# Flamingo cross-attention with a routed feed-forward: the fold's u in 48 jobs over the batches' borders, and m stored in longer and loaded in shorter packets

## The reference, cut to what matters

```python
# x (4, 2048, 512), ctx (4, 77, 512); 16 heads of 64
xn = layernorm(layernorm(x), gamma, beta)
q = (xn @ w_q) per head;  k, v = split(ctx @ w_kv) per head
attn = softmax(q * 64**-0.5 @ k.T)                    # 77 keys per head
x = x + tanh(g_xattn) * tanh(gate) * (attn @ v @ w_out + b_out)
y = layernorm(x)
probs = softmax(y @ gate_w.T + gate_b); top 2 of 10 (8 experts, 2 null), weights of true ones normalised
x = x + tanh(g_ffn) * sum over chosen e of weight * (y @ expert_w[e] + expert_b[e])
```

## Time and profile before

| what | value |
|---|---|
| median of 3 runs | 1552.9 us |
| the profiled execution's own time | 1539.97 us |
| its span in the trace | 1538.2 us |
| TensorE busy | 1336.4 us (87%) |
| VectorE busy | 1204.0 us (78%) |
| ScalarE busy | 785.8 us (51%) |
| GpSimd busy | 921.5 us (60%) |

### The profile page before, as it was taken

How to read it: one execution, slowest core, us unless ns; L and a number is a source line. 1 busy time by engine, 2 the same in 40 slices (tenths; PEclk the granted TensorE clock), 3 DMA queues, 4 the chain that set the end, 5 groups by cost and what they waited for, 6 DMA issues and landing times. The chain is left out here.

```text
span 1538.2 us, 31337 instructions
## 1 busy us (share of the span) xinstructions
PE 1336.4 (87%) x7241; PEld 685.0 (45%) x7242; DVE 1204.0 (78%) x2764; ACT 785.8 (51%) x2777; POOL 921.5 (60%) x781
## 2 busy tenths in 40 slices
PE   5676199999999999999999999998039998899997
PEld 4332054444444444444444444544015554455553
DVE  5766478899999999999999999996356775666765
ACT  5766266655555555565555555554024443344442
POOL 0450255557666766766776776674537775666664
PEclk9787699999999999999999999999569999999999
DMA  5795468889887788887788987777135442677773
GB/s 199 195 241 166 136 128 179 179 189 217 180 238 163 179 191 215 213 195 171 172 206 198 235 182 167 172 155 174 63 131 169 161 155 101 212 239 238 238 235 116
DMA packets 419892, 280.37 MB, mean 182 GB/s; under 512 B 325009, under 2 KB 352785, under 8 KB 419448
## 3 DMA queue, kind: packets, MB, share of 16 engines
q1 hardware_dynamic: 391992, 205.52, 55.1%
q0 software_dynamic: 27840, 74.18, 15.3%
HBM read 123.38 MB, written 83.07 MB: 134 GB/s over the span
## 5 line engine op out<-in xcount | busy, mean ns | idle before, releaser
L752 PE MATMUL scores<-m_sb,zT 128*128 (+2 forms) x2304 | 416.4, 339 | 43.3 <-DMA zT<-z_parts 31.2
L768 PE MATMUL mix<-u_sb,pT 128*128 128x512 f16 (+1 forms) x1920 | 425.0, 379 | 0.6 <-DVE x_out L947 0.6
L841 ACT ACTIVATE expd<-scores,less 128x77 f32<-128x77 f32 x1024 | 317.4, 329 | 203.4 <-DVE less L923 202.5
L1582 PE MATMUL out_bank<-w_parts,y_columns 128*128 x1440 | 335.7, 384 | 2.3 <-issue 2.2
L752 PEld LDWEIGHTS scores<-m_sb,zT 128*128 128x128 f16 x2304 | 223.6, 98 | 212.1 <-DMA zT<-z_parts 31.6
L768 PEld LDWEIGHTS mix<-u_sb,pT 128*128 128x128 f16 (+1 forms) x1920 | 187.8, 98 | 220.5 <-DVE x_out L947 0.8
L841 ACT ACTIVATION_READ_ACCUMULATOR expd<-scores,less 128x1 f32 x1024 | 213.9, 209 | 0.0
L1582 PEld LDWEIGHTS out_bank<-w_parts,y_columns 128*128 128x128 f16 x1440 | 142.2, 99 | 152.2 <-issue 13.6
L1247 POOL DMA_INDIRECT table<-payload,row_i x128 | 158.6, 1239 | 59.2 <-issue 34.7
L1605 ACT CAST y_columns<-yT_bank 128x512 f16<-128x512 f32 x120 | 70.2, 585 | 183.9 <-PE yT_bank L1569 183.9
L1224 POOL TENSOR_TENSOR z<-z,beta 128x512 f32<-128x512 f32 x64 | 152.0, 2376 | 5.0
(11 more groups left out here) (158 smaller groups left out, 1880.1 us busy)
## 6 DMA issues: line engine op xcount, KB each, us to landing
comb<-x_out SPq DMA_DIRECT2D x64, 512.0 KB, 3.2
x_ln<-in_x_dram SPq DMA_DIRECT2D x64, 256.0 KB, 2.7
x_res<-in_x_dram SPq DMA_DIRECT2D x64, 256.0 KB, 2.8
w_raw<-in_L_ffn_expert_w_dram SPq DMA_DIRECT2D x64, 128.0 KB, 2.3
m_dram<-m_stage SPq DMA_DIRECT2D x32, 231.0 KB, 5.7
u_dram<-m_sb SPq DMA_DIRECT2D x48, 154.0 KB
m_sb<-m_dram SPq DMA_DIRECT2D x12, 616.0 KB
u_sb<-u_dram SPq DMA_DIRECT2D x6, 1024.0 KB, 6.8
```

What stands on the lines that cost most here:

```text
L752: last = pe.matmul(scores[s][k][:, 0:n], zT[:, s, zp, t, :], m, start=(t == 0 and (zp, mp) == PRODUCTS[0]), stop=(t == DT - 1 and (zp, mp) ...
L768: last = pe.matmul(mix[:], pT[0:n, s, pp, k, :], u_sb[0:n, k, up, :], start=(k == 0 and (pp, up) == PRODUCTS[0]), stop=(k == KT - 1 and (p ...
L841: last = act.activation(expd[:, s, h * KEYS:(h + 1) * KEYS], scores[s][k][:, at:at + KEYS], ACT.Exp, bias=less[:, s, h:h + 1], scale=1.0 / ...
L1582: last = pe.matmul(c.out_bank[s][:], yT[:, s, yp, t, :], w_parts[:, bass.ds(e, 1), t, wp, :].rearrange("p a n -> p (a n)"), start=(t == 0 ...
```

## The change

It changes how u is cut into jobs and how m lies in DRAM.

- The four batches' 308 rows of one head lie side by side in `v_stack`. They are now cut at 128, so a head has three jobs, of 128, 128 and 52 rows, and the 16 heads have 48 jobs, ordered by head. A job's rows belong to up to three batches, and `u_pieces` cuts the store where a batch ends: job 0 holds the 77 rows of batch 0 (into `u_sb`, cut as before) and 51 of batch 1; job 1 holds 26 of batch 1, 77 of batch 2 and 25 of batch 3; job 2 holds 52 of batch 3. The slots get 128 rows.
- `m_dram` is laid out by row block, part, quad, row, batch, so that one store of a quad's part is 128 rows of 3·308·2 = 1848 contiguous bytes in place of 384 of 616 B. `m_stage` has the part ahead of the batch. The load of one batch's m takes two DMAs a row block, one for each part, of 512 pieces of 616 B each, in place of one DMA with 128 pieces of 4928 B. PE's count of landed loads is doubled.

```diff
 def load_m(engine, m_sb, m_dram, b, t):
-    return engine.dma_start(m_sb[:, :, t].rearrange("p a l c -> p (a l) c"),
-                            m_dram[bass.ds(b, 1), :, t].rearrange("a p l c -> (a p) l c"))
+    for part in range(2):
+        yield engine.dma_start(m_sb[:, :, t, part].rearrange("p a (q c) -> p (a q) c", q=QUADS),
+                               m_dram[t, part, :, :, bass.ds(b - 1, 1)].rearrange("q p a c -> p (q a) c"))
...
-    NU = BATCH * HEADS
+    CHUNKS = -(-CK // P)
+    NU = HEADS * CHUNKS
...
-        m_stage = sb("m_stage", [P, MS, BATCH, 2, 4 * KEYS], F16)
+        m_stage = sb("m_stage", [P, MS, 2, BATCH, 4 * KEYS], F16)
...
+        def chunk_rows(n):
+            return min(P, CK - n % CHUNKS * P)
...
         def u_pieces(n):
-            b, h = divmod(n, HEADS)
-            if b > 0:
-                return [(slice(0, KEYS), u_dram[b, h * KEYS:(h + 1) * KEYS])]
...
+            h, c = divmod(n, CHUNKS)
+            pieces = []
+            for b in range(BATCH):
+                first, end = max(b * KEYS, c * P), min((b + 1) * KEYS, c * P + chunk_rows(n))
+                if first >= end:
+                    continue
+                s0, s1 = first - c * P, end - c * P
+                row0, row1 = h * KEYS + first - b * KEYS, h * KEYS + end - b * KEYS
+                if b > 0:
+                    pieces.append((slice(s0, s1), u_dram[b, row0:row1]))
+                    continue
+                for k in range(row0 // P, (row1 - 1) // P + 1):
+                    p0, p1 = max(row0 - k * P, 0), min(row1 - k * P, P)
+                    j0, j1 = k * P + p0 - row0 + s0, k * P + p1 - row0 + s0
+                    pieces.append((slice(j0, j1), u_sb[p0:p1, k]))
             return pieces
...
-                sp.dma_start(m_sb[:, 0, dt, :, cols], m_stage[:, g % MS, 0]).then_inc(m_stored[g % MS], 16)
+                sp.dma_start(m_sb[:, 0, dt, :, cols], m_stage[:, g % MS, :, 0]).then_inc(m_stored[g % MS], 16)
                 for part in range(2):
-                    sp.dma_start(m_dram[1:, :, dt, part, cols].rearrange("b p c -> p b c"),
-                                 m_stage[:, g % MS, 1:, part]).then_inc(m_stored[g % MS], 16)
+                    sp.dma_start(m_dram[dt, part, quad], m_stage[:, g % MS, part, 1:]).then_inc(m_stored[g % MS], 16)
...
                 for part in range(2):
-                    last = pe.matmul(out[0:KEYS, :], v_stack[:, h, b * KEYS:(b + 1) * KEYS],
+                    last = pe.matmul(out[0:m, :], v_stack[:, h, c * P:c * P + m],
                                      kvw_parts[:, h // 4, part, h % 4, :], start=(h > 0 and part == 0), stop=(part == 1))
...
-    m_dram = nc.dram_tensor("m_dram", [BATCH, P, DT, 2, COLS], F16, kind="Internal").ap()
+    m_dram = nc.dram_tensor("m_dram", [DT, 2, QUADS, P, BATCH - 1, 4 * KEYS], F16, kind="Internal").ap()
```

More of the change, by code:

```diff
@@ L27 @@
 COLS = HEADS * KEYS
+QUADS = HEADS // 4
 KT = -(-COLS // P)
@@ L122, in fold_context @@
         v_stack = sb("v_stack", [P, HEADS, CK], F16)
-        m_stage = sb("m_stage", [P, MS, BATCH, 2, 4 * KEYS], F16)
-        u_stage = m_sb[0:KEYS, 1].rearrange("p t l c -> p (t l c)")[:, 0:US * 2 * D].rearrange(
+        m_stage = sb("m_stage", [P, MS, 2, BATCH, 4 * KEYS], F16)
+        u_stage = m_sb[:, 1].rearrange("p t l c -> p (t l c)")[:, 0:US * 2 * D].rearrange(
             "p (u l n) -> p u l n", u=US, l=2)
@@ L129, in fold_context @@
         bias_parts = sb("bias_parts", [1, 2, D], F16)
-        ones_row = sb("ones_row", [1, KEYS], F16)
+        ones_row = sb("ones_row", [1, P], F16)
         gates = sb("gates", [P, 2])
@@ L184, in job @@
                 cols = slice(hh * KEYS, (hh + 1) * KEYS)
-                hi = m_stage[:, g % MS, :, 0, cols]
-                return [(hi, m_stage[:, g % MS, :, 1, cols], hi,
+                hi = m_stage[:, g % MS, 0, :, cols]
+                return [(hi, m_stage[:, g % MS, 1, :, cols], hi,
                          bank[:, 0:CK].rearrange("p (b j) -> p b j", b=BATCH),
                          M_SCALE * DH ** -0.5 / (K_SCALE * W16))]
-            u = (n - U0) % US
-            return [(u_stage[:, u, 0], u_stage[:, u, 1], u_stage[:, u, 0], bank[0:KEYS, :], u_gain[0:KEYS, :])]
+            u, m = (n - U0) % US, chunk_rows(n - U0)
+            return [(u_stage[0:m, u, 0], u_stage[0:m, u, 1], u_stage[0:m, u, 0], bank[0:m, :], u_gain[0:m, :])]
+        def chunk_rows(n):
+            return min(P, CK - n % CHUNKS * P)
         def u_pieces(n):
-            b, h = divmod(n, HEADS)
-            if b > 0:
-                return [(slice(0, KEYS), u_dram[b, h * KEYS:(h + 1) * KEYS])]
[L198 to L202, removed]
+            h, c = divmod(n, CHUNKS)
[13 more added lines that the diff above has]
+                    pieces.append((slice(j0, j1), u_sb[p0:p1, k]))
             return pieces
@@ L321, in _ @@
             for n in range(NU):
[L322 to L326, removed]
+                h, c = divmod(n, CHUNKS)
+                if c == 0 and h % 4 == 0:
+                    pe.wait_ge(chunk_hi_ready, 4 + h // 4 + 1)
+                    pe.wait_ge(wout_lo_ready, h // 4 + 1)
+                out, m = bank(U0 + n), chunk_rows(n)
                 if h == 0:
                     for part in range(2):
-                        pe.matmul(out[0:KEYS, :], ones_row[:], bias_parts[:, part], start=(part == 0), stop=False)
+                        pe.matmul(out[0:m, :], ones_row[:, 0:m], bias_parts[:, part], start=(part == 0), stop=False)
                 for part in range(2):
-                    last = pe.matmul(out[0:KEYS, :], v_stack[:, h, b * KEYS:(b + 1) * KEYS],
+                    last = pe.matmul(out[0:m, :], v_stack[:, h, c * P:c * P + m],
                                      kvw_parts[:, h // 4, part, h % 4, :], start=(h > 0 and part == 0), stop=(part == 1))
@@ L718, in batch @@
                     if not last:
-                        load_m(sp, m_sb[:, bass.ds((b + 1) % 2, 1)], m_dram, b + 1, k).then_inc(m_in, 16)
+                        for load in load_m(sp, m_sb[:, bass.ds((b + 1) % 2, 1)], m_dram, b + 1, k):
+                            load.then_inc(m_in, 16)
                     step(i0 + TPB - 4 + k, k % 2)
@@ L742, in score @@
                     if later(i, TPB):
-                        pe.wait_ge(m_in, 16 * DT * (i // TPB))
+                        pe.wait_ge(m_in, 32 * DT * (i // TPB))
                 for k in banks:
```

## The result

The changed kernel takes 1560.6 us, the median of 20 runs (1553.1 to 1568.2), against 1553.65 of the kernel before in 20 runs beside it (1549.9 to 1562.2). The ratio is 1.0046, 95% interval 1.0031 to 1.0061: slower by 7 us, within the 1% that I called no change. In a later session it was 1.0056 (1.0041 to 1.0070).

What follows compares the result with a forecast made beforehand. Prediction: DMA engines bound the fold, in the u stage the first engine's rows; matmuls bound attend. Terms +18.8 − 5 + 0.5 = +14.3 us on 1552.9 gave 1567.2 us (+0.9%), range 1556 to 1578.

Steps and rivals of the forecast that it cites:

- rival 4: Whole kernel: no change to speak of, m stores gain 9.6, u rows cost +14.8, sum +5.2 us, 1558.1; chance 0.12.
- u stores, +18.8: End of the fold: first engine's rows go from 577 to 801 at 92 ns each, +18.8 us, bounds +14.8 and +22.0.
- It can't be hidden.: u stage: the first engine never runs dry and the fold's end waits for it, so the +18.8 us shows in full.
- reading of rows 6: u stores' DMA packets: small ones are end marks; engines used are the largest divisor of the row count up to 16.
- What the u jobs save, counted at nothing: u stage: 16 fewer jobs save 10.6 us of DVE, but beside the first engine's 73.7 us, so nothing counted.
- m stores, −5: m stage of the fold: longer packets into DRAM save 5 us, bounds 1 and 9.6.
- so it counts in full: From m to u stage: the first engine starts on u that much sooner, so the whole 5 us gain counts.
- m loads, +0.5: Attend: loads of m in 616 B pieces cost 0.5 us, bounds 0 and 11.
- Carrying the difference to the median: Whole time: the profiled execution stands 12.9 us under the median of runs; that difference was kept for the forecast.
- What would show it: Profile after: first attend load about 184, ACT's u-store waits far over 16.7 us, u-stage DMA share from 0.66 towards 0.35.

Runs made afterwards that it cites:

- u part alone: The change's 48 u jobs, with m stored and loaded as in the kernel before; ratio 1.0079 to the kernel before.
- worse cut: The changed kernel with each u store of 51 rows cut into 17 and 34 rows; one run, 1565.0 us beside 1537.2 for the kernel before.
- m part alone: The change's m layout, stores and loads, with the old u jobs of the kernel before; ratio 0.9973 to the kernel before.
- the old order: Kernel before with the new m layout, 64 u jobs by batch; with batch 0's five badly dividing stores cut, one run, 1580.2 us beside 1575.9.
- the order by head: Kernel before with the new m layout, its 64 u jobs ordered by head, then batch; ratio 0.9972, with five batch-0 stores cut 0.9932.
- even cut: The changed kernel with u stores of 51, 53, 76, 23 or 74 rows cut into a multiple of 16 rows and the rest; ratio 1.0039 to the kernel before.

## Why the prediction was right or wrong

The direction, the place and the bound hold: 7 us slower within a range of 1556 to 1578, 5.9 to 6.8 of it in the fold, by more rows on the first engine, less what the m stores give. The size doesn't: +14.3 forecast, +7 measured, and the range holds it because it reaches down to rival 4. Rival 4, which I gave 0.12, has about the right sum (+5.2) but not the right terms: +14.8 and −9.6, where the runs with one part each show +10.0 and −4.1 at the fold's end. That its sum fits is luck.

- **u stores, +18.8.** Mis-sized, and the step that failed. The u part alone moves the fold's end by 10.0 us (its timed runs say 9.8 to 14.4), and the stage goes from 59.7 to 70.3: below my lower bound of +14.8. Two things were wrong. First the price of a row: the worse cut gives 73 ns for each row added, not 92. I had taken it from a stretch with eleven engines at work (96) and from a phase that SP's issuing also bounded (94). But 224 rows at 73 ns are still 16.4 us. So, second, the stage before: I took all of it as the first engine's 577 rows, and 53.1 against 54.9 us seemed to prove it. At 73 ns they are 42 us. In its first phase SP's 21.1 us of issues stand beside the engine's rows, so I read it that some of the new rows fell into time in which that engine had nothing to do. How the difference splits between the two wasn't measured, nor what the rest of the changed stage's 70.3 us is beyond 801 rows at 73 ns, 58 us.
- **"It can't be hidden."** Held for the fold's end, which moved by what the stage did, in every run; that the first engine never runs dry is shown for neither kernel. The reading of rows 6 (marks, divisors) held too, to 20 of 972 small packets. That the rows left fall on the same engine each time, which no row named, is shown by the worse cut.
- **What the u jobs save, counted at nothing.** Held, in that no saving shows. SP's 53.8 us I had put under the first engine's 73.7; it is a near bound, since with the rows evened out, and 21 more issues, the stage only falls from 70 to 68 us.
- **m stores, −5.** The m part alone gives −4.1, so the number was good, but by a step that failed: "so it counts in full". The engines were free of m at about 105 in place of 114.5 (112.5 in the second profile), the whole −9.6 of my upper bound against the first profile and −7.5 against the second. Only 4.1 of that reached the fold's end. SP's first store of u moved from 108.3 to 104.0, 4.3 us, and the old u stage took its 59.5 to 60 us from that store on as before. The short packets were what made the slow spells: at 1848 B the rate is 340 GB/s.
- **m loads, +0.5.** Held: attend 859.7 against 859.6, SP's loads at 0.40 us each, below the 0.8 that I had allowed.
- **Carrying the difference to the median.** This let the forecast stand on a single fold, which was 2 us longer than in the next profile. Against the first profile the fold's end moves by only 3.7 us, against the second by 5.9, and the runs measure 7.
- **What would show it.** ACT's waits went as said. The first load of attend came at 174, not 184. The DMA share fell to 0.53, not 0.35: the busy time of a packet isn't fixed (152 GB/s at 0.53 is 18 GB/s an engine, against 21 before), so a share can't be scaled by bytes.

## What to carry to other kernels

When a tile is stored in pieces, count for each piece the largest divisor of its row count up to 16, and add up the rows that fall on the first engine: by that count a piece of 53 rows puts all 53 on it, one of 48 rows only 3. Then add up the issues of the queue that sends them. Evening out the rows alone gave 0.5 us in the old order, 1.6 in the changed kernel and 5.5 in the order by head; evening them out and taking the stores into `u_sb` off SP together gave 18 (174.1 to 155.7). Here 16 jobs fewer cost 10 us, because each head's stores then fell into pieces of 51, 26, 25 and 52 rows: fewer jobs pay only if the pieces that result aren't worse to store. And a stage's gain is to be read against two profiles of the old kernel, since one of them can be 2 us off in the very stage.

## What the runs showed of the hardware

- SP issues stores from on-chip memory into `u_sb` 0.79 to 0.84 us apart and stores into DRAM 0.41 us apart, with little effect of their size (in the even cut 0.29 us for one of 3 rows into DRAM, 0.35 for one of 77). GpSimd's instruction for the former lasts 0.53 us.
- A row of 2048 B added to the busiest engine cost 73 ns in the worse cut, 28 GB/s, though the mean busy time of such packets was 96 ns with eleven engines at work.
- 1848 B in place of 616 B packets into DRAM, for the same bytes, raised the rate of a stretch with all engines busy from 307 to 340 GB/s and the mean of the m stage from 242 to 302, and took away spells at 208.
- Loading in 616 B pieces what was loaded in 4928 B ones, 7.6 MB in all, cost attend nothing that shows.
- The expert stage of one program took from 397 to 436 us in two profiles, with all before it equal to 2 us.
